# Attention in a two-layer kernel: four of 16 half tiles of probabilities a head are turned by DMA

## The reference

```python
# x [1, 1024, 256]; layer 0: x + attention(xn) * silu(mixture_of_experts(xn)), layer 1 likewise
q, k, v = (einsum('bse,ehd->bshd', xn, w) for w in (wq, wk, wv))       # 16 heads, 128 each
scores = einsum('bqhd,bkhd->bhqk', rms_norm(q, q_scale), rms_norm(k, k_scale))
attn = softmax(scores, axis=-1)                                          # not causal
out = einsum('bhqk,bkhd->bqhd', attn, v)
return einsum('bqhd,hde->bqe', out, wo)
```

## Time and profile before

| | us | share |
|---|---|---|
| median of three runs | 1142.44 | |
| the profiled execution | 1143.51 | |
| its span, first to last instruction | 1141.7 | 100% |
| TensorE matmuls busy | 1031.2 | 90% |
| VectorE busy | 824.4 | 72% |
| ScalarE busy | 623.7 | 55% |
| GpSimd busy | 579.8 | 51% |
| attention, by the first and the last head's scale stores | 180.8 to 765.6 | about half of the span |

### The profile page before, as it was taken

One profiled execution on the slowest core, in us unless ns is written; L12 is line 12 of the kernel. 1 busy time (PEld: TensorE's weight loads), 2 busy tenths in 40 slices (PEclk: granted clock), 3 DMA queues, 4 the chain that ended last, 5 costly groups with the idle time before them and its releaser, 6 DMA issues. The chain is left out here.

```text
span 1141.7 us, 21617 instructions
## 1 busy us (share of the span) xinstructions
PE 1031.2 (90%) x7790; PEld 688.7 (60%) x7790; DVE 824.4 (72%) x1461; ACT 623.7 (55%) x1225; POOL 579.8 (51%) x449
## 2 busy tenths in 40 slices
PE   5976989999999999999999999989978878979797
PEld 4455766666666666666666666548724345557434
DVE  3878257877887888788778887954589955866467
ACT  3564166666666666666666666742441025646532
POOL 3222457557765875587558754534148202621263
PEclk9965999999999999999999999989999978989899
DMA  5664023667677656775776567651102326759833
GB/s 176 114 199 143 2 56 65 64 104 81 92 73 104 77 93 77 104 80 88 77 101 81 87 65 91 80 133 43 57 37 79 106 89 211 223 169 299 285 90 93
DMA packets 196543, 122.34 MB, mean 107 GB/s; under 512 B 75044, under 2 KB 189782, under 8 KB 196182
## 3 DMA queue, kind: packets, MB, share of 16 engines
q1 hardware_dynamic: 178934, 97.74, 47.9%
q10 hardware_dynamic: 14432, 14.81, 3.9%
q0 software_dynamic: 3072, 8.39, 2.2%
HBM read 81.90 MB, written 36.37 MB: 104 GB/s over the span
## 5 line engine op out<-in xcount | busy, mean ns | idle before, releaser
L1293 DVE TENSOR_REDUCE a_nmax<-psum 128x1 f32<-128x1024 f32 x128 | 156.3, 1221 | 81.6 <-PE psum L1141 78.3
L1299 DVE SCALAR_TENSOR_TENSOR a_pT<-psum,a_pT 128x512 f16<-128x512 f32 x256 | 163.8, 682 | 18.5 <-ACT a_pT L1236 13.7
L1236 ACT ACTIVATE a_pT<-psum 128x512 f16<-128x512 f32 x256 | 139.7, 603 | 14.1 <-PE psum L1152 13.0
L1059 POOL TENSOR_TENSOR a_rnorm<-a_ss,a_power 128x8 f32<-128x8 f32 x32 | 57.6, 1800 | 171.4 <-DVE a_ss L1269 171.2
L1228 ACT ACTIVATE a_ex<-psum,a_nmax 128x1024 f32<-128x1024 f32 x128 | 142.8, 1116 | 0.3 <-DVE a_nmax L1293 0.2
L1152 PEld LDWEIGHTS psum<-ident,a_ex 128*128 128x128 f32 x1024 | 120.5, 141 | 25.1 <-issue 0.7
L1152 PE MATMUL psum<-ident,a_ex 128*128 128x128 f32 x1024 | 133.4, 273 | 0.0
L1123 PE MATMUL psum<-a_wh,xT_h 128*128 128x128 f16 (+1 forms) x512 | 115.3, 248 | 2.0 <-PEq L2738 2.0
L1124 PE MATMUL psum<-a_wl,xT_h 128*128 128x128 f16 (+1 forms) x512 | 115.3, 248 | 0.0
L1125 PE MATMUL psum<-a_wh,xT_l 128*128 128x128 f16 (+1 forms) x512 | 115.2, 248 | 0.0
L1163 PE MATMUL psum<-a_pT,a_vh 128*128 128x512 f16 x256 | 98.1, 383 | 6.4 <-DVE a_of L977 5.1
(11 more groups left out here) (397 smaller groups left out, 2531.9 us busy)
## 6 DMA issues: line engine op xcount, KB each, us to landing
split_gate_up<-a_e_wh SPq DMA_DIRECT2D x64, 128.0 KB
a_rb<-row_scales SPq DMA_DIRECT2D x32, 256.0 KB
g_e_gu<-split_gate_up SPq DMA_DIRECT2D x32, 256.0 KB, 3.9
block_outputs<-g_e_ym ACTq DMA_DIRECT2D x16, 512.0 KB, 4.5
split_rest<-a_e_wh SPq DMA_DIRECT2D x45, 128.0 KB
wf<-in_L_ffn_W_gate SPq DMA_DIRECT2D x32, 128.0 KB, 2.5
wf<-in_L_ffn_W_up SPq DMA_DIRECT2D x32, 128.0 KB, 2.5
wf<-in_L_ffn_W_down SPq DMA_DIRECT2D x32, 128.0 KB, 3.0
```

Of the source, the lines that this page charges most:

```text
L1236: act.activation(pT[g][:, 0, 4 * h:4 * h + 4, (m % 4) * P:(m % 4 + 1) * P], bank_of(r, unit).rearrange("p (k q) -> p k q", k=4), ACT.Copy, ...
L1293: dve.tensor_reduce(nmax[:, k:k + 1], score_banks(m), AX.X, ALU.max, negate=True).then_inc(max_ready, 1)
L1299: dve.scalar_tensor_tensor(low, bank_of(r, unit).rearrange("p (k q) -> p k q", k=4), PROB, high, ALU.mult, ALU.subtract).then_inc(low_done, 1)
```

## The change

Per head, the half tiles (m, 1) of m = 0, 2, 4 and 6 are no longer transposed by TensorE. Their high and low f16 parts are made straight from `ex` (two SBUF operands for VectorE), at the end of step m - 1, into `halves`, which lie in the room of `x`; a DMA transpose on the sync queue turns both parts into `pT`, whose layout is changed so that the parts alternate block by block. The third piece of a group's values waits for its two turned halves. The sync program has another order: the four turns stand in it, the second group's scale load comes at the start of the next head, its store after the third chunk, and the last head's `wo` loads come behind the last turn. `x` is loaded again after the last turn, and `add_up` waits for it. The split halves of a chunk are laid out so that high and low of an expert are adjacent: two stores instead of three, with rows twice as long (three times for the rest chunks).

```diff
@@ -746,7 +746,9 @@
-        self.halves = [tmp(f"e1_wh{b}", [P, 2, self.WIDTH], F16) for b in range(2)]
+        halves = [tmp(f"e1_wh{b}", [P, 2 * self.WIDTH], F16) for b in range(2)]
+        self.blocks = [x[:, :].rearrange("p (i a d) -> p i a d", a=2, d=D) for x in halves]
+        self.parts = [x[:, :].rearrange("p (a c) -> p a c", a=2) for x in halves]
@@ -808,12 +810,18 @@
-        whole = self.wf[b][:, :]
-        lift = self.lift.to_broadcast([P, self.WIDTH])
-        high, low = self.halves[b][:, 0, :], self.halves[b][:, 1, :]
+        t, j = k // 3, k % 3
+        if j < 2:
+            whole = self.wf[b][:, :].rearrange("p (i d) -> p i d", d=D)
+            lift = self.lift.unsqueeze(2).to_broadcast([P, self.WIDTH // D, D])
+            high, low = (self.blocks[b][:, :, part, :] for part in range(2))
+        else:
+            whole = self.wf[b][:, :]
+            lift = self.lift.to_broadcast([P, self.WIDTH])
+            high, low = (self.parts[b][:, part, :] for part in range(2))
-        if not (isinstance(uses, int) and uses == 1):
-            pool.wait_ge(self.stored[b], 48 * uses - 48)
+        if uses > 1:
+            pool.wait_ge(self.stored[b], 32 * uses - 32)
@@ -828,14 +836,13 @@
+            sp.dma_start(self.gu[two, :, :, :].rearrange("e p a x -> p e (a x)"),
+                         self.blocks[b][:, 0:2, :, :].rearrange("p e a x -> p e (a x)")).then_inc(self.stored[b], 16)
+            sp.dma_start(self.dn[two, :, :, :].rearrange("e f a d -> (e f) (a d)"),
+                         self.blocks[b][:, 2, :, :].rearrange("p a d -> p (a d)")).then_inc(self.stored[b], 16)
+        else:
-                sp.dma_start(self.gu[two, :, part, :].rearrange("e p x -> p e x"),
-                             self.halves[b][:, part, 0:2 * self.GU].rearrange("p (e x) -> p e x", e=2)).then_inc(self.stored[b], 16)
-            sp.dma_start(self.dn[two, :, :, :].rearrange("e f a d -> (e f) a d"), self.halves[b][:, :, 2 * self.GU:])\
-              .then_inc(self.stored[b], 16)
-        else:
-            for at in range(0, self.WIDTH, D):
-                sp.dma_start(self.rest[:, :, t * self.WIDTH + at:t * self.WIDTH + at + D], self.halves[b][:, :, at:at + D])\
+                sp.dma_start(self.rest[:, part, t * self.WIDTH:(t + 1) * self.WIDTH], self.parts[b][:, part, :])\
@@ -844,7 +851,7 @@
-            sp.wait_ge(done, 48 * len(range(b, chunks, 2)))
+            sp.wait_ge(done, 32 * len(range(b, chunks, 2)))
@@ -858,6 +865,7 @@
+    BY_DMA = [(m, 1) for m in (0, 2, 4, 6)]
@@ -880,7 +888,7 @@
-            made += [("tile", m, h) for h in range(2)]
+            made += [("tile", m, h) for h in range(2) if (m, h) not in BY_DMA]
@@ -933,13 +941,18 @@
-        pT = [tmp(f"pT{b}", [P, 2, KT, HALF], F16) for b in range(2)]
+        pT = [tmp(f"pT{b}", [P, KT, 2, HALF], F16) for b in range(2)]
+        room = env["x"][:, :, :].rearrange("p n d -> p (n d)").bitcast(F16)
+        halves = [room[:, b * 2 * HALF:(b + 1) * 2 * HALF].rearrange("p (k a q) -> p k a q", a=2, q=P)
+                  for b in range(len(BY_DMA))]
...
+        p_high, p_low = sem("a0_ph"), sem("a0_pl")
+        p_turned = [sem(f"a0_pt{b}") for b in range(len(BY_DMA))]
@@ -954,9 +967,39 @@
+        def tiles_at(m):
+            return [("tile", m, h) for h in range(2) if (m, h) not in BY_DMA]
+        def halves_next(t, m):
+            u, coming_m = (t, m + 1) if m < QT - 1 else (t + 1, 0)
+            return [(u, i) for i, (at, _) in enumerate(BY_DMA) if at == coming_m and u < H]
...
+        def pieces_of(m, h):
+            return slice(4 * h, 4 * h + 4), slice(4 * h * P, (4 * h + 4) * P), slice((m % 4) * P, (m % 4 + 1) * P)
+        def split_count(t, i):
+            return len(BY_DMA) * t + i + 1
+        def turn_half(sp, t, i):
+            m, h = BY_DMA[i]
+            blocks, _, cols = pieces_of(m, h)
+            sp.wait_ge(p_low, split_count(t, i))
+            if t > 0:
+                sp.wait_ge(pv_ready, 2 * t + m // 4 - 1)
+            sp.dma_start_transpose(pT[m // 4][:, blocks, :, cols].rearrange("p k a q -> p (k a) q"),
+                                   halves[i].rearrange("p k a q -> p (k a q)")).then_inc(p_turned[i], 16)
+        def wait_turned(engine, t, g):
+            for i, (m, _) in enumerate(BY_DMA):
+                if m // 4 == g:
+                    engine.wait_ge(p_turned[i], 16 * t + 16)
@@ -994,7 +1037,16 @@
-        env["last_half"] = (last_scales, split_stored, last_high, last_low, o_low, 2 * H)
+        def load_tokens(sp):
+            for g in range(2):
+                wait_turned(sp, H - 1, g)
+            tokens = w["L0_attn_x"][0].rearrange("(n p) d -> p n d", p=P)
+            for i, loaded in enumerate(env["x_loaded"]):
+                tiles = slice(i * X_TILES, (i + 1) * X_TILES)
+                sp.dma_start(env["x"][:, tiles, :], tokens[:, tiles, :]).then_inc(loaded, 16)
+        env["last_half"] = (last_scales, split_stored, last_high, last_low, o_low, 2 * H, load_tokens)
@@ -1012,29 +1064,40 @@
                 load(2)
                 for k in range(2):
                     experts.load(sp, k)
+                def next_chunk(k):
+                    experts.store(sp, k)
+                    if k == 3 * (H - 2) + 1:
+                        experts.wait_stored(sp, 18)
+                    if k + 2 < 3 * H:
+                        experts.load(sp, k + 2)
                 for t in range(H):
+                    turn_half(sp, t, 0)
                     if t + 3 < H:
                         load(t + 3)
+                    if t > 0:
+                        load_scales(sp, t - 1, 1)
+                    turn_half(sp, t, 1)
                     store_scales(t, 0)
-                    if t == H - 1:
+                    if t < H - 1:
+                        next_chunk(3 * t)
+                        turn_half(sp, t, 2)
                         load_scales(sp, t, 0)
+                        next_chunk(3 * t + 1)
+                        turn_half(sp, t, 3)
+                        next_chunk(3 * t + 2)
+                    else:
+                        turn_half(sp, t, 2)
+                        load_scales(sp, t, 0)
+                        turn_half(sp, t, 3)
                         sp.wait_ge(ss_ready, 2 * H)
                         sp.wait_ge(made, unit_count(H - 2, ("side", 1, NS - 1)))
                         for part, dst in enumerate(env["wo_halves"]):
                             sp.dma_start(dst.rearrange("p h e -> p (h e)"), env["split_rest"][:, part, 0:H * D])\
                               .then_inc(wo_loaded, 16)
-                    for j in range(3):
-                        if j == 1 and t < H - 1:
-                            load_scales(sp, t, 0)
-                        if j == 2:
-                            store_scales(t, 1)
-                        experts.store(sp, 3 * t + j)
-                        if t == H - 2 and j == 1:
-                            experts.wait_stored(sp, 18)
-                        if 3 * t + j + 2 < 3 * H:
-                            experts.load(sp, 3 * t + j + 2)
-                    if t < H - 1:
-                        load_scales(sp, t, 1)
+                        for j in range(3):
+                            next_chunk(3 * t + j)
+                    store_scales(t, 1)
                 sp.wait_ge(wo_loaded, 32)
             @block.gpsimd
@@ -1157,9 +1220,11 @@
+                    if piece == 2:
+                        wait_turned(pe, t, g)
...
-                        ph, pl = (pT[g][:, part, k, :] for part in range(2))
+                        ph, pl = (pT[g][:, k, part, :] for part in range(2))
@@ -1172,7 +1237,7 @@
-                        for h in range(2):
+                        for _, _, h in tiles_at(m):
@@ -1222,7 +1287,10 @@
-                        act.wait_ge(made, unit_count(t, ("tile", m - 2, 1)) if m >= 2 else unit_count(t - 1, ("tile", QT + m - 2, 1)))
+                        u, past = (t, m - 2) if m >= 2 else (t - 1, QT + m - 2)
+                        act.wait_ge(made, unit_count(u, tiles_at(past)[-1]))
+                        if (past, 1) in BY_DMA:
+                            act.wait_ge(p_low, split_count(u, BY_DMA.index((past, 1))))
@@ -1233,8 +1301,19 @@
-                    act.activation(pT[g][:, 0, 4 * h:4 * h + 4, (m % 4) * P:(m % 4 + 1) * P],
-                                   bank_of(r, unit).rearrange("p (k q) -> p k q", k=4), ACT.Copy, scale=PROB).then_inc(high_done, 1)
+                    blocks, _, cols = pieces_of(m, h)
+                    act.activation(pT[g][:, blocks, 0, cols], bank_of(r, unit).rearrange("p (k q) -> p k q", k=4), ACT.Copy,
+                                   scale=PROB).then_inc(high_done, 1)
+                def half_high(t, i):
+                    m, h = BY_DMA[i]
+                    _, keys, _ = pieces_of(m, h)
+                    if t > 0:
+                        act.wait_ge(p_turned[i], 16 * t)
+                    act.wait_ge(exp_ready, QT * t + m + 1)
```

(25 more changed lines are left out.)

## The result

The changed kernel takes 1152.48 us (median of 5 runs, 1148.96 to 1156.99), the kernel before 1142.6 beside it (1142.22 to 1143.23). The ratio is 1.0089 with a 95% interval of 1.0068 to 1.011: slower by 0.9%, some 10 us. The profiled execution has a span of 1150.8 us, against 1141.7.

A forecast was written before the change was run, and what follows sets the result against it. TensorE is busy but meets VectorE twice a head with almost nothing to spare. Fourteen heads at 0.35 give +4.9, the end -1.9 and -1: +2, so 1145.5 profiled and 1144 us as median; range 1121 to 1156.

The forecast's parts named there:

- likeliest case: Whole kernel: VectorE's path takes back the removed transposes, about +0.35 us a head; own range 1139 to 1148, chance 0.45.
- What bounds a head: Attention: TensorE is busy, but twice a head meets VectorE with almost nothing to spare; about +0.35 us a head, not -1.76.
- point A: First values of step 4: step 2's saving is lost and the new conversion delays the values from 415.60 to 415.99, +0.39 us.
- from A to B: From step 4's values to the next head's step 0 values (second meeting point): those start at 434.6, against 434.25.
- early conversion: VectorE's low conversion of a DMA-turned half, one step earlier in steps 7, 1, 3, 5: 0.6 us, bounds 0.6 and 1.5.
- mostly near 0.9: Sign of being right: VectorE's small multiply (L1306) in steps 3 and 7 takes mostly near 0.9 us, blocked by GpSimd.
- upper bound of 1.5 us: Longest time given for the new VectorE conversion, which starts just after a GpSimd instruction of 1.47 us.
- The end: Last heads: -1.9 us as a turn separates the scale load from two 1 MB loads; about -1 for the last two heads.
- rival D: Sync queue: second group's scale store leaves about 5 us later; margin 2 to 4 us; if exceeded, 1159 to 1175; chance 0.17.
- The reload of `x`: First addition: reload due some 4 us late, but TensorE's first token turn needing it comes three projections later: nothing.
- B (the multiply slips in ahead of GpSimd): Steps 3 and 7: VectorE's small multiply comes before GpSimd's instruction, a head costs about 37.1 us; 1124 us, chance 0.25.
- C: Whole kernel: TensorE stays the bound everywhere and all 28 us of removed transposes come; 1114 us, chance 0.07.

The follow-up runs named there:

- e10: Changed kernel with only the second halves of tiles 2 and 6 turned by DMA, scale row and room in `x` as in e6 and e7: 1150.04 us, ratio 1.0022.
- e11: As e10, but with the halves of tiles 0 and 4 in place of 2 and 6: 1158.23 us, ratio 1.009.
- e9: Changed kernel, still four halves a head, without the small multiply, with scale row and room in `x` as in e6 and e7: 1156.36 us, ratio 1.0074.
- e12: As e10 (tiles 2 and 6 by DMA), but also without the small multiply: 1144.97 us, ratio 0.9966.
- e2: Changed kernel with the four conversions made in the step of their own tile, behind `finished`, not one step ahead: 1177.13 us, ratio 1.0308.
- e3: Changed kernel with the edits of e1 and e2 together: 1148.11 us, ratio 1.0044.
- e8: Changed kernel with the second halves of tiles 1, 3, 5, 7 turned by DMA instead of those of 0, 2, 4, 6: 1151.96 us, ratio 1.0098.
- e6: Changed kernel with each head's second scale row stored ahead of the third chunk, as in the kernel before: 1152.91 us, ratio 1.0095.
- e7: Changed kernel with the halves in two buffers in the second half of `x`, so only token tiles 4 to 7 are reloaded: 1148.1 us, ratio 1.0051.
- e1: Changed kernel without the small multiply ahead of the reciprocal, its factor PROB moved into `finished`: 1136.19 us, ratio 0.9928.

## Why the prediction held, and where not

The time lay in the range (1121 to 1156), but 8.5 us above the forecast of 1144 and above the likeliest case's own 1139 to 1148. The mechanism was that case's; the size of the tail was not.

- **What bounds a head.** Right. TensorE looked like the bound, and 1.76 us a head less for it gave +0.37 for the head; I had +0.35. The two halves of a head say the same of the parts: +0.38 up to point A in every head, where I had +0.39, and -0.01 from A to B, where I had -0.04. TensorE's waits were 0.90 us in step 4 of every head and 0.77 on average in step 0, where I had 1.1 and 0.8. Point A came out by its own working; at B two small errors offset (the multiply of step 7 took 0.32 us more than before over the full heads where I had 0.45, the conversion 0.68 where I had 0.6).
- **The parts of it.** The early conversion was taken at 0.6 us and took 0.68 and 0.77 ahead of `finished`, 0.80 on average, within its bounds. L1396 stayed blocked, in step 3 of most heads for 1.37 us. That is just what the working says (reached at 410.46, released at 411.83), because it is reached 0.44 earlier and let go by the same GpSimd instruction; the sign "mostly near 0.9" in the last paragraph of the prediction doesn't follow from its own working. I had priced no effect on L1025, the other VectorE operation with two SBUF operands; it grew from 0.90 to 1.33 us, but VectorE has idle time between it and the next meeting point (1.32 us before 428.03 in the head shown), so it doesn't count.
- **The conversions as cause.** The heads with equal multiplies in e10 and e11, and e9 beside e12, bear it out; e2, e3 and e8 show that the step could not be mended by moving them, because their price depends on GpSimd. The upper bound of 1.5 us held in the changed kernel (1.14 at most), but not in those places: up to 2.37 us in e2 and e3 and 2.0 in e8, in e3 beside a GpSimd instruction of 1.90 us, where the bound was made from one of 1.47.
- **The end.** Here the sum failed. I had -1.9 for a scale load that no longer shares with two 1 MB loads and -1 for the last two heads. From step 3 of the last head but one to step 3 of the last it took 30.4 us, 0.5 more than before, and not less. The stretch to the projection came out +1.6: TensorE waited 5.7 us in step 4 of the last head for the second scale row of the head before. That is rival D's mechanism, which didn't occur in the full-length heads, but did in the last, whose steps are shorter; with the row stored earlier (e6) the stretch is 24.5 us. The wait for the last head's own first row fell from 4.7 to 1.3, more than the 1.9 I had given it. I had checked D's margin with a full-length head, and not with the short one.
- **The reload of `x`.** Taken at nothing, since the first token turn on TensorE comes three projections later. The addition itself stood 7.3 us, VectorE's work piled up behind it, and the projection took 2.3 us more; e7 takes exactly that away. The cover I named was real for one consumer and not for the queue behind it.
- **The rest** (+1.7 behind the projection) is of the size by which executions of the changed kernel differ (1149 to 1157), and in the 14 traces this stretch lies between 322 and 329 us; it isn't explained.
- **Rivals.** B (the multiply slips in ahead of GpSimd) didn't occur. e1, without the block, has 36.92 us as its commonest head and 37.49 as its mean, where I had 37.1 for B. In e6 and e10 the multiply was free (0.16 us) in step 3 of 12 and of all 14 steady heads, and they got no shorter, 38.79 us, with ScalarE's stall in nearly all of them. C was never near. D was right once in sixteen heads.
- **The sign.** The forecast was +2 us on the profiled execution, below what I said a measurement can tell, with 0.39 for slower and 0.40 for faster. Of the 9.1 us measured, the heads gave 4.8, as forecast; the sum had -3 for the rest, which came out at +4.3. That the loss is clear of noise was not foreseen; the range of 35 us was wide enough to take it in.

## What to carry over

An engine that is 99% busy is not the bound of a loop if another one reaches a shared meeting point just in time; take the work away from the first and the second appears. Before moving VectorE work that reads two SBUF operands, or a tiny `tensor_scalar`, look at what GpSimd does in that very step: the same instruction cost 0.68 us in one step and 2.4 in another. And check each margin of a queue in the shortest iteration of the loop, the last, too.

## What was not expected of the hardware

- A 128x4 multiply on VectorE took 0.16 us when free and up to 1.38 us when it started during a GpSimd instruction (up to 1.60 in e11); the reciprocal of the same columns 0.166 to 0.169 in e1. The kernel before without its 32 such multiplies was 0.9% faster (0.6 to 1.3%).
- Behind a 2 KB store of 4-byte elements the DMA engines stay busy and move almost nothing for 6 to 8 us (under 30 GB/s from 476 to 484 in e12; 11 to 28 GB/s from 473 to 479 in the kernel before, where 379 of the 439 packets were under 512 bytes), and issues behind it take 3.6 us for two and 5.2 for one, instead of 1.3 and 0.6 (e6).
- The kernel before ran at medians of 1140.9, 1143.9 and 1147.8 us on three chips.
